# A one-core vision block in float32: set-up loads split over two queues, the set-up's order changed, the first pixel sums made to wait

## What is computed

```python
# tokens: 4 by 4 patches, the mean of a patch asks, its 16 pixels answer
x = features.reshape(b, c, h, s, w, s)
reduce_feats = x.mean((3, 5)).reshape(b, c, hw).transpose(0, 2, 1)
unf = x.transpose(0, 1, 2, 4, 3, 5).reshape(b, c, hw, n).transpose(0, 2, 3, 1)
q = _ln(reduce_feats, ln_q_w, ln_q_b) @ Wq.T
kv = _ln(unf, ln_kv_w, ln_kv_b) @ Wkv.T
attn = softmax(einsum('bhpd,bhpnd->bhpn', q * scale, k))
h = reduce_feats + einsum('bhpn,bhpnd->bhpd', attn, v) @ proj_w.T + proj_b
# attention over 256 tokens in chunks of 128, with a decay per head
scores = einsum('bhcd,bhed->bhce', qi, ki) * mask      # mask = exp(-slope * distance), lower triangle
h = layernorm(h + attention(h) @ w_proj + b_proj)
# two of eight experts per token, then a layer norm
h = layernorm(h + moe(h))
```

## Time and profile before

| | us |
|---|---|
| median of 3 runs | 2413.96 |
| lowest, highest | 2413.16, 2414.79 |
| the profiled execution | 2413.36 |
| its span | 2411.6 |
| TensorE busy in the span | 2253.4 (93%) |
| VectorE, ScalarE, GpSimd busy | 1882.0, 1772.0, 1885.6 |

### The profile page before, as it was taken

The page is one execution under the profiler, slowest core; times in us unless marked ns, Lnnn a source line. Parts: engine busy times, 40 slices in busy tenths (PEclk is TensorE's granted clock), DMA queues, the critical chain, the costliest instruction groups (busy, mean ns, idle before and its releaser), DMA issues. The chain is left out here.

```text
span 2411.6 us, 89169 instructions
## 1 busy us (share of the span) xinstructions
PE 2253.4 (93%) x31921; PEld 1015.0 (42%) x31921; DVE 1882.0 (78%) x4131; ACT 1772.0 (73%) x4281; POOL 1885.6 (78%) x2077
## 2 busy tenths in 40 slices
PE   0799999999999999999999999999999977999997
PEld 0344444444444444444444444444444442222222
DVE  5588888888788888888888888888888867777775
ACT  0888888888888888888888888888888734555554
POOL 3599999999999999999999999999999741333333
PEclk9999999999999999999999999999999978999999
DMA  4333333333333333333333333333333100100001
GB/s 84 72 72 72 73 78 76 76 73 72 72 72 72 72 72 72 74 77 76 76 72 72 72 71 72 72 72 72 74 78 76 25 1 5 23 22 22 22 22 27
DMA packets 573777, 147.82 MB, mean 61 GB/s; under 512 B 573504, under 2 KB 573504, under 8 KB 573504
## 3 DMA queue, kind: packets, MB, share of 16 engines
q1 hardware_dynamic: 573504, 143.53, 29.9%
HBM read 135.10 MB, written 8.39 MB: 59 GB/s over the span
## 5 line engine op out<-in xcount | busy, mean ns | idle before, releaser
L600 ACT ACTIVATE xd<-xb 128x512 f32<-128x512 f32 x512 | 586.1, 1178 | 0.0
L885 DVE TENSOR_TENSOR kqs<-ps,qqT 128x512 f32<-128x512 f32 x512 | 352.8, 689 | 286.5 <-PE ps L394 280.0
L389 PE MATMUL ps<-xd,w_ckv 64*64 64x512 f32 x2048 | 551.6, 615 | 7.5 <-ACT sqs L582 5.5
L394 PE MATMUL ps<-xd,w_ckv 64*64 64x512 f32 x2048 | 551.6, 615 | 0.0
L714 POOL TENSOR_TENSOR pv<-vs,aw 128x512 f32<-128x512 f32 x512 | 534.8, 1077 | 0.0
L582 ACT ACTIVATE sqs<-ps 128x512 f32<-128x512 f32 x512 | 307.6, 601 | 196.3 <-PE ps L394 196.2
L772 POOL TENSOR_TENSOR xt<-xb 128x512 f32<-128x512 f32 x256 | 323.5, 1289 | 58.0 <-DMA xb<-in_x_dram 35.1
L896 DVE TENSOR_TENSOR sm<-ps,decay 128x1024 f32<-128x1024 f32 x256 | 301.3, 1219 | 28.7 <-PE ps L473 24.8
L724 POOL TENSOR_TENSOR pv<-pv 128x512 f32<-128x512 f32 x256 | 322.2, 1283 | 0.0
L416 PE MATMUL ps<-w_ckv,xd 64*64 64x64 f32 x16384 | 297.9, 221 | 0.0
L416 PEld LDWEIGHTS ps<-w_ckv,xd 64*64 64x64 f32 x16384 | 263.5, 135 | 49.5 <-issue 34.4
(11 more groups left out here) (225 smaller groups left out, 3910.3 us busy)
## 6 DMA issues: line engine op xcount, KB each, us to landing
xb<-in_x_dram SPq DMA_DIRECT2D x512, 256.0 KB, 4.3
out_dram<-outb SPq DMA_DIRECT2D x128, 64.0 KB, 1.6
w1p<-in_L_ffn_w_dram SPq DMA_DIRECT2D x16, 16.0 KB
w2p<-in_L_ffn_w_dram SPq DMA_DIRECT2D x8, 16.0 KB
b1p<-in_L_ffn_b_dram SPq DMA_DIRECT2D x8, 0.2 KB
b2v<-in_L_ffn_b_dram SPq DMA_DIRECT2D x8, 2.0 KB
sm<-in_L_tok_Wkv_dram SPq DMA_DIRECT2D x4, 16.0 KB, 2.1
w_av<-in_L_attn_w_qkv_dram SPq DMA_DIRECT2D x4, 16.0 KB, 2.2
```

What stands on the lines that cost most here:

```text
L389: nc.tensor.matmul(KB[own, :], w_ckv[own, 2 * P + m * C:2 * P + (m + 1) * C], xd[own, j, :], start=True, stop=True)
L394: mm = nc.tensor.matmul(CB[(1 - m) * C:(2 - m) * C, :], w_ckv[own, m * C:(m + 1) * C], xd[own, j, :], start=True, stop=True)
L600: nc.scalar.activation(xd[:, j, :].rearrange("p (b t) -> p b t", b=ST), xb[:, f, :].rearrange("p (b t d) -> p d b t", b=ST, d=ST)[:, j], A ...
L885: V.tensor_tensor(kqs[:, j, :].rearrange("p (b t) -> p b t", b=ST), KB.rearrange("p (b t) -> p b t", b=ST), qqT[:, s, :].unsqueeze(1).to_b ...
```

## The change

It changes the set-up alone.

- The 28 set-up loads stand in two lists. SyncE issues the 14 of loads[0]; ScalarE issues the 14 of loads[1] behind its table load and a wait for s_zero. The x loads of SyncE so stand behind 14 loads, not 28.
- VectorE's wait for ld_w moves down: 14 operations that read no loaded tile, and the five that make the centring parts of `w_ckv`, `w_qc` and `w_av` from `ident` and `blockmask`, stand ahead of it.
- ScalarE's activations wait for a new semaphore, s_slope, which VectorE raises when `nsl` and the two copies of it in `scr` are written. The two copies of `bp_row` come after these.
- GpSimd waits for s_dve0 = 1 ahead of its first pixel sum.

```diff
--- before.py
+++ after.py
@@ -202,6 +202,7 @@
             s_set = sem("s_set")
             s_dve0 = sem("s_dve0")
             s_act0 = sem("s_act0")
+            s_slope = sem("s_slope")
             s_pe0 = sem("s_pe0")
             x_in = [sem("x_in%d" % r) for r in range(4)]
             kc_pe = sem("kc_pe")
@@ -276,33 +277,37 @@
             def row(ap, n):
                 return ap.unsqueeze(0).to_broadcast([P, n])
 
+            loads = ([
+                (rows[0:64, 0, :], Wq), (rows[64:128, 0, :], Wq),
+                (rows[0:64, 1, :], Wkv[0:64, :]), (rows[64:128, 1, :], Wkv[0:64, :]),
+                (rows[0:64, 2, :], Wkv[64:128, :]), (rows[64:128, 2, :], Wkv[64:128, :]),
+                (rows[0:64, 3, :], proj_w), (rows[64:128, 3, :], proj_w),
+            ], [
+                (slb[:], row(slopes, 8)), (bprow64[:], row(b_proj, 64)),
+                (lnb[:, 0, :], row(ln_q_w, 64)), (lnb[:, 1, :], row(ln_q_b, 64)),
+                (lnb[:, 2, :], row(ln_kv_w, 64)), (lnb[:, 3, :], row(ln_kv_b, 64)),
+            ])
+            for m in range(2):
+                half = slice(64 * m, 64 * m + 64)
+                loads[0].extend([
+                    (w_av[half, 0:C], w_qkv[:, 128:192]),
+                    (w_av[half, C:2 * C], w_qkv[:, 64:128]),
+                    (rt[half, m * E:(m + 1) * E], router_w.rearrange("e c -> c e")),
+                ])
+                loads[1].extend([
+                    (pb_col[half, :], proj_b.unsqueeze(1)),
+                    (w_aq[half, 64 * m:64 * m + 64], w_qkv[:, 0:64]),
+                    (w_ak[half, 64 * m:64 * m + 64], w_qkv[:, 64:128]),
+                    (w_ap[half, CR * m:CR * m + C], w_proj),
+                ])
+            assert len(loads[0]) + len(loads[1]) == LOADS
+
             @block.sync
             def _(sp):
 
                 sp.wait_ge(s_zero, 9)
-                todo = [
-                    (rows[0:64, 0, :], Wq), (rows[64:128, 0, :], Wq),
-                    (rows[0:64, 1, :], Wkv[0:64, :]), (rows[64:128, 1, :], Wkv[0:64, :]),
-                    (rows[0:64, 2, :], Wkv[64:128, :]), (rows[64:128, 2, :], Wkv[64:128, :]),
-                    (rows[0:64, 3, :], proj_w), (rows[64:128, 3, :], proj_w),
-                    (lnb[:, 0, :], row(ln_q_w, 64)), (lnb[:, 1, :], row(ln_q_b, 64)),
-                    (lnb[:, 2, :], row(ln_kv_w, 64)), (lnb[:, 3, :], row(ln_kv_b, 64)),
-                    (bprow64[:], row(b_proj, 64)), (slb[:], row(slopes, 8)),
-                ]
-                for m in range(2):
-                    r = slice(64 * m, 64 * m + 64)
-                    todo += [
-                        (pb_col[r, :], proj_b.unsqueeze(1)),
-                        (w_aq[r, 64 * m:64 * m + 64], w_qkv[:, 0:64]),
-                        (w_av[r, 0:C], w_qkv[:, 128:192]),
-                        (w_av[r, C:2 * C], w_qkv[:, 64:128]),
-                        (w_ak[r, 64 * m:64 * m + 64], w_qkv[:, 64:128]),
-                        (w_ap[r, CR * m:CR * m + C], w_proj),
-                    ]
-                    todo += [(rt[r, m * E:(m + 1) * E], router_w.rearrange("e c -> c e"))]
-                for dst, src in todo:
+                for dst, src in loads[0]:
                     sp.dma_start(dst, src, allow_slow_non_contiguous=True).then_inc(ld_w, 16)
-                assert len(todo) == LOADS
 
                 def load(i, r):
 
@@ -557,7 +562,10 @@
             def _(act):
 
                 nc.scalar.preload_act_table_set('natural_log_exp_and_others')
-                act.wait_ge(s_dve0, 1)
+                act.wait_ge(s_zero, 9)
+                for dst, src in loads[1]:
+                    act.dma_start(dst, src, allow_slow_non_contiguous=True).then_inc(ld_w, 16)
+                act.wait_ge(s_slope, 1)
                 for h in range(HEADS):
                     nc.scalar.activation(decay[:, h, :], diff[:], ACT.Exp, scale=nsl[:, h:h + 1])
                 nc.scalar.activation(kdec[:], nsl[:], ACT.Exp, scale=pos[:, 1:2])
@@ -762,6 +770,8 @@
                                                     rden[:, 1 - s, :].unsqueeze(2).to_broadcast([P, SL, D]),
                                                     ALU.mult).then_inc(agg_done, 1)
 
+                    if isinstance(i, int) and 4 * i + r == -2:
+                        pool.wait_ge(s_dve0, 1)
                     if there(i, r, -2):
                         f = (r + 2) % 4
                         H = PX // 4
@@ -788,7 +798,6 @@
             def _(dve):
 
                 dve.wait_ge(s_pool0, 7)
-                dve.wait_ge(ld_w, 16 * LOADS)
                 link, n = chain(dve, s_set, 0)
                 V = nc.vector
                 link(V.memset(ssq[:], 1.0))
@@ -805,10 +814,19 @@
                 link(V.tensor_scalar(diff[:], diff[:], 0.0, None, ALU.max))
                 link(V.tensor_copy(pos[:, 0:1], posi[:]))
                 link(V.tensor_scalar(pos[:, 1:2], pos[:, 0:1], -1.0, float(P), ALU.mult, ALU.add))
+                link(V.scalar_tensor_tensor(w_ckv[:, 0:P], blockmask[:], -1.0 / C, ident[:], ALU.mult, ALU.add))
+                for m in range(2):
+                    h = slice(m * C, (m + 1) * C)
+                    link(V.tensor_scalar(w_qc[h, C:2 * C], w_ckv[h, m * C:(m + 1) * C], 1.0 / N, None, ALU.mult))
+                    link(V.tensor_scalar(w_av[h, 2 * C:3 * C], w_ckv[h, m * C:(m + 1) * C], 1.0 / N, None, ALU.mult))
+
+                dve.wait_ge(ld_w, 16 * LOADS)
                 link(V.tensor_scalar(nsl[:], slb[:], -1.0, None, ALU.mult))
                 for m in range(2):
-                    link(V.tensor_copy(scr[:, 2, m * C:(m + 1) * C].rearrange("p (h d) -> p h d", d=D),
-                                       nsl[:].unsqueeze(2).to_broadcast([P, HEADS, D])))
+                    ins = V.tensor_copy(scr[:, 2, m * C:(m + 1) * C].rearrange("p (h d) -> p h d", d=D),
+                                        nsl[:].unsqueeze(2).to_broadcast([P, HEADS, D]))
+                ins.then_inc(s_slope, 1)
+                for m in range(2):
                     link(V.tensor_copy(bp_row[:, m * CR:m * CR + C], bprow64[:]))
 
                 for j, b_at, dst in ((0, 1, col[:, 0:1]), (1, 3, col[:, 1:2]), (2, 3, bv_col[:])):
@@ -830,12 +848,6 @@
                 link(V.tensor_copy(bq_c[:], col[:, 0:1]))
                 link(V.tensor_copy(scr[:, 0, :], col[:, 0:1].to_broadcast([P, P])))
                 link(V.tensor_scalar(selbk[:], headmask[:], col[:, 1:2], WS, ALU.mult, ALU.mult))
-                link(V.scalar_tensor_tensor(w_ckv[:, 0:P], blockmask[:], -1.0 / C, ident[:], ALU.mult, ALU.add))
-                for m in range(2):
-                    h = slice(m * C, (m + 1) * C)
-                    link(V.tensor_scalar(w_qc[h, C:2 * C], w_ckv[h, m * C:(m + 1) * C], 1.0 / N, None, ALU.mult))
-                    link(V.tensor_scalar(w_av[h, 2 * C:3 * C], w_ckv[h, m * C:(m + 1) * C], 1.0 / N, None, ALU.mult))
-
                 for t in (w_ap, bp_row):
                     th = t[:].rearrange("p (m c) -> p m c", c=CR)[:, :, 0:C]
                     link(V.tensor_reduce(col[:, 4:6], th, AX, ALU.add))
```

## The result

The changed kernel takes 2395.49 us (median of 4 runs, 2393.08 to 2396.6), against 2414.37 for the kernel before beside it (4 runs, 2413.16 to 2414.79): the ratio is 0.9921, with a 95% interval of 0.9904 to 0.9938. That is 18.9 us faster, where 23.8 were forecast. The time is inside the range of 2387.5 to 2395.5 by 0.01 us and above the forecast's own range, 2388 to 2392. The profiled execution took 2394.99, its span is 2393.3.

A forecast was written before the change was run, and what follows sets the result against it. TensorE bounds the loop, so only the set-up ahead of its first query at 60.45 us can go. 8.0 + 3.0 + 2.5 + 11.1 + 0.7 - 1.5 - 0 = 23.8 us off 2413.96 gives 2390.2; range 2387.5 to 2395.5.

The forecast's parts named there:

- a late queue: Rival, chance 0.10: late x loads of unit 4 overrun the slack by 2 to 3 us, reaching TensorE: 2392.2 to 2393.2.
- a second queue that issues slowly: Rival, chance 0.14: ScalarE's queue issues set-up loads slower or shares a limit; 2398.2 if all 8.0 us go, 2393.1 in between.
- Loads on two queues: Set-up loads split over SyncE and ScalarE: VectorE gets its weights at 14.05 instead of 22.05, 8.0 us saved.
- Operations ahead: VectorE's 14 operations and five of `w_ckv` finish before the set-up loads land: 3.0 + 2.5 us saved.
- Pixel sums: GpSimd's first sums wait for VectorE's set-up chain, whose operations then run unslowed: 11.1 us saved, the largest term.
- Exponentials: ScalarE's set-up exponentials run beside VectorE, so TensorE's idle time before the transpose of `qd_tok` goes: 0.7 us saved.
- The moved sums: GpSimd's later pixel sums fall beside VectorE's second chain and may hold two SBUF operations: 1.5 us lost.
- The late queue, 0: Term for unit 4's x loads on SyncE: 2.3 us late, covered by slack with 0.1 to spare, so 0 lost.
- The slower rival: Rival, chance 0.03: the loop's engines settle in another lock, each of 124 units paying; at 0.30 us each, 2427.

The follow-up runs named there:

- the later single one: The changed kernel run once more with nothing altered, for a second trace: 2396.98 us (1 run).

## Why the prediction was right and where it was wrong

That the time lies inside the range is in part luck. The set-up's terms came out, and a little more; but the forecast's 23.8 missed by 4.9, and the range of 2387.5 to 2395.5 holds 2395.49 only because it was widened for a late queue priced at 2392.2 to 2393.2, and for a second queue that issues slowly, which did not occur. Two of the four runs (2395.99, 2396.6) and the later single one (2396.98) lie above it.

- **Loads on two queues, 8.0: right.** ScalarE issues at 0.62 per load, against the 0.61 taken; `nsl` is at 13.87, against 14.05 (the wait for the loads ended at 22.05 before). Undone with everything else free, it is 7.8. The rival of a slow second queue fell. The Trainium skill's "usually small" (DMA: Bandwidth & Descriptors, on issuing engines not being separate DMA queues) does not hold in this set-up, where 28 loads of at most 32 KB cost 17 us of one sequencer.
- **Operations ahead, 5.5: right**, as far as it was measured: all of them back behind the wait, beside a GpSimd at rest, makes 4.3 (the 3.0 and the unslowed 1.3); the remaining 1.2 is the slowing of the five of `w_ckv`, which the pixel sums' wait removes as well.
- **Pixel sums, 11.1: right.** From `nsl` to its end, without the part of `w_ckv`, the chain takes 11.3 us against 22.6 before, and it ended at 25.16, against 25.5. Freeing them costs 9.8, though they then meet only a part of the chain.
- **Exponentials, 0.7: right** (0.67 of idle time gone; undone, the transpose starts 0.93 later).
- **The moved sums, 1.5: about half.** One of the two operations was held, by 0.71, and the other not at all; from s_dve0 to the first query it takes 10.10 now, against 10.32 before and 11.1 in the sum. Together with the 0.4 of the chain this makes the shift 25.2 instead of 23.8.
- **The late queue, 0: the step that failed.** The prediction had the mechanism, in its order: x loads late, the sum of unit 4 late, `pv` behind it, `vs` at the end. It wrote "So 2.3 is covered with 0.1 to spare". The lateness was 6.0, 3.7 more than the 2.3 it had: 1.4 from the larger shift, which the queue does not share; 0.3 from the 16 x loads (17.89 against 17.61); 1.2 from the expert loads, 25.5 us now for 24.3 before; 0.8 between the last of them and the first x load. A margin of 0.1 under a backlog of 40 loads, whose end differed by 0.7 between two executions of the change (56.21 and 56.91), was no margin; the forecast should have been the late queue's case. It also took `vs` of unit 3 for the first to be reached; at 5.8 late, with 2.9 of slack, it was already that of unit 2.
- **Its price in the rival, 2392.2 to 2393.2 for an overrun of 2 to 3 us, was mis-sized**: the overrun of 2.9 came through as 2.6 at TensorE, as worked out, and then cost 4.05 more by the clock. That TensorE's clock could fall was in no part of the sum. The shift of 25.2 less 6.7 gives 18.5, and 18.3 were found at the end of the span.
- **The slower rival** (a new lock, each unit a little longer) fell: in the loop GpSimd is busy 371.27 of 400 us and TensorE 393.42, as before, and the shift goes only from 18.8 at unit 5 to 18.3 at the last query.

The medians of the three versions with all, four or two of the expert loads behind are 23.5 to 24.4 us below the kernel before, for a shift of 25 at the first query and 22.8 to 24.7 in the loop: about the forecast's 23.8 is what the change gives once the queue is out of its way.

What stays open: four runs of one kernel differ by 1.1 to 6.0 us (six with the set-up loads on one queue), those of the kernel before by 1.6, but its 13 runs in the last series by 3.5; that the change spreads more is not shown. A part of the spread arises after the last unit: from the last query to the end of the span the thirteen traces take 495.4 to 497.7 us without an order by kernel (495.7 before, 495.6 and 497.0 in the two of the change). Around the gap between the two blocks the granted clock is low, 0.50 to 0.75 from 1940 to 2020 us in the kernel before. What makes the difference there is open. TensorE's clock was not moved by itself either: its share of the loss is read from how long the same matmuls take.

## What to carry to other kernels

When the start of a pipeline is moved forward, go through every queue and ask what of its backlog does not move with it: the gain ends where the first buffer is refilled from a queue that kept its old end. A slack that covers the lateness by a tenth is not to be trusted; take loads that nobody needs for a millisecond out of such a queue, even if the move is worth nothing in the kernel as it stands. And price a rest of TensorE twice, once as the wait and once as the clock, which here added 1.4 to 4.05 us to waits of 2.6 to 4.25.

## What the runs showed of the hardware

- A rest of TensorE of 2.45 us, after one of 1.28 us shortly before, came with a granted clock of 0.68, 0.50 and 0.80 in three windows of 5 us and a loss of 4.05 us; rests of 3.46 and 4.05 us came with a similar fall. In all three the fall began within the rest. A rest of 1.37 us was followed by a fall in one execution (0.83), and one of 1.39 us at the same place by a fall in a second (0.66) and by none in a third (1.00).
- GpSimd and VectorE hold each other up in turn: the pair of pixel sums at 30.55 took 3.46 us instead of 2.49, and line 871, which began within it at 30.96, 1.93 instead of 1.22. The Trainium skill (SBUF — State Buffer, section SBUF: two separate sides) has this as a lock that the one who starts first holds for the whole instruction, and both rows agree with it.
- Which VectorE operations are held is not a matter of size. With the sums free to start, a 128x64 product took 1.24 beside them and eight 128x64 copies 0.82 each on average, instead of 0.23; a reduction of 128x64 and a scaling of one element per partition kept their 0.22 and 0.15.
- The queue of one engine issues the same loads at slightly different speeds: the last four of the expert loads took 2.65 and 2.99 us in two executions of the change and 1.49 before. Why is open.
